# GpSimd makes the block division and the product back of a rounded feed-forward

## What is computed

```
def _mx_quantize(t, eps=1e-30):
    rows, K = t.shape
    blocks = t.reshape(rows, K // BLOCK_SIZE, BLOCK_SIZE)
    scales = jnp.maximum(jnp.max(jnp.abs(blocks), axis=-1) / FP6_E2M3_MAX, eps)
    q = _nearest_on_grid(blocks / scales[..., None], _GRID)
    return (q, scales)

x = x + _L2_xattn_ref(_layernorm(x, axis=-1), ctx_1024, mask, ...)
x = x + _L2_ffn_ref(_layernorm(x, axis=-1), L2_ffn_weight, L2_ffn_bias)
x = x + _L3_xattn_ref(_layernorm(x, axis=-1), ctx_1024, ctx_1024, ...)
```

## Time and profile before

| | us |
|---|---|
| median of 3 executions | 1220.91 (1218.79 to 1223.61) |
| the profiled execution | 1221.49 |
| its span (first to last instruction) | 1219.7 |
| PE busy | 1064.2 |
| DVE busy | 867.1 |
| ACT busy | 814.3 |
| GpSimd busy | 811.6 |

### The profile page before, as it was taken

The page is one execution under the profiler, slowest core; times in us unless marked ns, Lnnn a source line. Parts: engine busy times, 40 slices in busy tenths (PEclk is TensorE's granted clock), DMA queues, the critical chain, the costliest instruction groups (busy, mean ns, idle before and its releaser), DMA issues.

```text
span 1219.7 us, 32093 instructions
## 1 busy us (share of the span) xinstructions
PE 1064.2 (87%) x12044; PEld 880.3 (72%) x12044; DVE 867.1 (71%) x2068; ACT 814.3 (67%) x1691; POOL 811.6 (67%) x899
## 2 busy tenths in 40 slices
PE   7999896999997877787799899988778999996895
PEld 5777775999995555456588777767676777776795
DVE  8898982442226898988255587899977999986442
ACT  3577665877767989873332268877547798984573
POOL 6677788582523888678745867784346677756765
PEclk9899987999998899986899989999899999998998
DMA  6135202475326323301375400000030000001451
GB/s 214 54 113 175 55 24 80 147 215 168 105 66 193 98 80 104 97 21 49 96 227 169 99 16 15 19 26 21 17 98 27 20 28 19 28 2 53 137 155 36
DMA packets 101048, 102.59 MB, mean 84 GB/s; under 512 B 14348, under 2 KB 79120, under 8 KB 100896
## 3 DMA queue, kind: packets, MB, share of 16 engines
q1 hardware_dynamic: 90176, 78.15, 21.4%
q0 software_dynamic: 10720, 22.39, 6.4%
HBM read 57.79 MB, written 43.16 MB: 83 GB/s over the span
## 4 chain that ended last, share of the span: by engine, by line
PE 23%; DVE 11%; POOL 9%; issue 5%; ACT 3%; DMA 1%; POOLq 0%; ACTq 0%; DVEq 0%; SPq 0%
POOL F_xbuf L3016 3%; PE bP L1201 2%; POOL uni L2860 2%; PE bS L1263 2%; PE bS L1010 2%; PE bP L1019 1%; DVE mx L2339 1%; PE b L1030 1%; PE bS L859 1%; DVE uni L2151 1%; PE b L1189 1%; DVE mx L2155 1%; PE bS L1189 1%; POOL gb L3056 1%; PE bP L1278 1%
## 5 line engine op out<-in xcount | busy, mean ns | idle before, releaser
L2860 POOL TENSOR_TENSOR uni<-uni,mx 128x1024 f32<-128x1024 f32 x96 | 183.8, 1914 | 95.7 <-DVE mx L2155 65.2
L3016 POOL DMA_INDIRECT F_xbuf<-rows,idxS x128 | 132.8, 1037 | 55.3 <-issue 25.7
L2800 POOL DMA_INDIRECT gb<-F_ybuf,idxG x104 | 109.2, 1050 | 59.2 <-PE b L763 23.9
L884 PEld LDWEIGHTS b<-Vall,uni 128*64 128x64 f32 x3072 | 105.0, 144 | 42.0 <-ACT uni L1395 21.2
L884 PE MATMUL b<-Vall,uni 128*64 128x18 f32 x3072 | 110.8, 215 | 26.9 <-ACT uni L1395 14.4
L1389 ACT ACTIVATE uni<-uni 128x1024 f32<-128x1024 f32 x96 | 101.4, 1056 | 40.4 <-POOL uni L2860 39.8
L859 PE MATMUL bS<-uni,Qx 64*64 64x256 f32 x1536 | 112.2, 410 | 16.9 <-ACT uni L1352 11.1
L870 PE MATMUL bP<-k_ident,uni 128*128 128x128 f32 x768 | 110.0, 290 | 9.4 <-ACT uni L1389 9.2
L1395 ACT ACTIVATE uni<-bP 128x512 f32<-128x512 f32 x192 | 104.9, 596 | 16.2 <-PE bP L870 14.5
L870 PEld LDWEIGHTS bP<-k_ident,uni 128*128 128x128 f32 x768 | 91.0, 149 | 19.8 <-ACT uni L1389 17.3
L859 PEld LDWEIGHTS bS<-uni,Qx 64*64 64x64 f32 x1536 | 52.0, 139 | 58.7 <-issue 25.6
(11 more groups left out here) (373 smaller groups left out, 2993.2 us busy)
## 6 DMA issues: line engine op xcount, KB each, us to landing
F_xbuf<-zero SPq DMA_DIRECT2D x9, 514.0 KB, 4.9
uni<-F_xbuf SPq DMA_DIRECT2D x9, 514.0 KB, 4.7
uni<-F_xbuf SPq DMA_DIRECT2D x18, 256.0 KB, 3.4
F_ybuf<-uni SPq DMA_DIRECT2D x18, 256.0 KB
uni<-ctx_dram SPq DMA_DIRECT2D x32, 128.0 KB, 3.2
A_keys<-Qx SPq DMA_DIRECT2D x16, 256.0 KB, 2.3
uni<-A_keys SPq DMA_DIRECT2D x16, 256.0 KB
uni<-A_keys SPq DMA_DIRECT2D x32, 128.0 KB
```

The source lines that it names most:

```text
L884: ins = T.matmul(b7[64 * b:64 * b + 64, 144 * i + 18 * c:144 * i + 18 * c + 18], pPT[t % 2][:, 128 * c + 64 * b:128 * c + 64 * b + 64], pV ...
L2800: G.indirect_dma_start(gb[n], None, rows_, bass.IndirectOffsetOnAxis(ap=idxG[:, t, c:c + 1], axis=0)).then_inc(*gathered[n].up)
L2860: g.raises(G.tensor_tensor(s3, s3, mx3[t % 3][:, :].unsqueeze(2).to_broadcast([128, 16, 64]), ALU.subtract), b_sb, L, t)
L3016: G.indirect_dma_start(SP[L][0], bass.IndirectOffsetOnAxis(ap=idxS[:, t, c:c + 1], axis=0), rows3[:, t, :] if L == "F3" else XA[:, t, :], ...
```

## The change

GpSimd makes the division of each block (pool_scaled) and the product back (pool_rounded), and DVE's L2666 and L2686 are gone. Two semaphores are new: q_sc (DVE's reciprocal is there) and q_rd (DVE's last rounding step is there); q_z and q_out are now raised by GpSimd. The scales get a third buffer, am[B % 3], and DVE's scaled(B) waits for q_out(B - 3) ahead of its first instruction. Where the division and the product stood, DVE's generator has an empty step, so that its pace in A2 stays. Four tables and three calls say where in its program GpSimd does its 16 new instructions.

```
-        am = [sb(f"am{i}", [128, 64]) for i in range(2)]
+        am = [sb(f"am{i}", [128, 64]) for i in range(3)]
...
             def scaled(B):
-                z, m = steps_of(B)[0], am[B % 2]
+                z, m = steps_of(B)[0], am[B % 3]
                 d.wait_ge(f_xn, L, B)
+                d.wait_ge(q_out, L, B - 3)
...
-                n = d.tick(V.reciprocal(m[:, 32:48], m[:, 16:32]))
+                V.reciprocal(m[:, 32:48], m[:, 16:32]).then_inc(*q_sc.up)
                 yield
-                d.after(n)
-                V.tensor_tensor(blk(z), blk(z), over(m[:, 32:48]), ALU.mult).then_inc(*q_z.up)
                 yield
...
-                n = d.tick(V.scalar_tensor_tensor(a, g, MAGIC / 8.0, z, ALU.max, ALU.subtract, reverse1=True))
+                V.scalar_tensor_tensor(a, g, MAGIC / 8.0, z, ALU.max, ALU.subtract, reverse1=True).then_inc(*q_rd.up)
                 yield
-                d.after(n)
-                V.tensor_tensor(blk(g), blk(a), over(am[B % 2][:, 16:32]), ALU.mult).then_inc(*q_out.up)
                 yield
...
+        SCALED2, SCALED3 = {21: 0, 25: 1, 31: 2, 35: 3, 38: 4}, {-4: 6, -3: 7}
+        TURNED2, TURNED3 = {28: (0,), 33: (1,), 36: (2,)}, {-3: (5,), -2: (6, 7)}
+
+        def pool_scaled(g, B):
+
+            z = steps_of(B)[0].rearrange("p (n k) -> p n k", k=32)
+            g.wait_ge(q_sc, "F2", B)
+            g.alone()
+            g.raises(G.tensor_tensor(z, z, am[B % 3][:, 32:48].unsqueeze(2).to_broadcast([128, 16, 32]), ALU.mult), q_z, "F2", B)
+
+        def pool_rounded(g, B):
+
+            a, to = (t.rearrange("p (n k) -> p n k", k=32) for t in steps_of(B)[1:])
+            g.wait_ge(q_rd, "F2", B)
+            g.alone()
+            g.raises(G.tensor_tensor(to, a, am[B % 3][:, 16:32].unsqueeze(2).to_broadcast([128, 16, 32]), ALU.mult), q_out, "F2", B)
...
                 if tile(s):
                     SB(s)
+                if kind == 2 and s in SCALED2:
+                    pool_scaled(g, SCALED2[s])
+                if kind == 2 and s in TURNED2:
+                    for B in TURNED2[s]:
+                        pool_rounded(g, B)
...
         def pool_cross(g, L):
+            pool_rounded(g, 3)
+            pool_scaled(g, 5)
+            pool_rounded(g, 4)
             g.wait_ge(b_AV, "A2", NT - 1)
...
             for s in range(-8, NT + 9):
+                for B in TURNED3.get(s, ()):
+                    pool_rounded(g, B)
+                if s in SCALED3:
+                    pool_scaled(g, SCALED3[s])
```

More of the change, by code:

```diff
@@ L324, in build @@
         f_dn, f_yo = sig("f_dn", F0=NS, F1=16, F3=NS3), sig("f_yo", F0=NGF, F1=16, F3=GL3 + sum(n for _, n in GROUPS3[GL3:]))
-        q_nm, q_z, q_ab, q_out, q_Y, q_xr = (sig(n, F2=NBK) for n in ("q_nm", "q_z", "q_ab", "q_out", "q_Y", "q_xr"))
+        q_nm, q_sc, q_z, q_ab, q_rd, q_out, q_Y, q_xr = (
+            sig(n, F2=NBK) for n in ("q_nm", "q_sc", "q_z", "q_ab", "q_rd", "q_out", "q_Y", "q_xr"))
         n_fx, n_xs, n_nx = (sig(n, F3=NP) for n in ("n_fx", "n_xs", "n_nx"))
@@ L2643, in blk @@
                 return t.rearrange("p (n k) -> p n k", k=32)
-            def over(t):
-                return t.unsqueeze(2).to_broadcast([128, 16, 32])
             def offset(B):
```

## The result

| | median, us | runs | lowest to highest |
|---|---|---|---|
| kernel before | 1221.25 | 21 | 1215.62 to 1226.01 |
| changed kernel | 1225.87 | 21 | 1219.70 to 1234.09 |

The ratio is 1.0039, 95% interval 1.0022 to 1.0055: 4.6 us slower, within the 0.5% that I had called no change, and 3.5 us above the forecast of 1222.4. It is also 0.9 us above the 1220 to 1225 that I had given the forecast's own case. The profiled run of the changed kernel was the longest of its 21, 1234.09 us with a span of 1232.3, so its trace shows more than the median lost. For that reason I measure between landmarks inside the traces: from one instruction to the same one further on.

A forecast was written before the change was run, and what follows sets the result against it. GpSimd was full until A2's step 24, DVE fullest to 865 us, PE the limit in F2's tail. Division 4 +2.05, clock +1.5, block 7 -0.7 and -1.4 gave +1.45 us: 1222.4 us, range 1215.5 to 1228.

The forecast's parts named there:

- The case that I held likeliest: Whole kernel: division 4 makes PE late in F2's tail, most else is covered; +1.45 us, 1220 to 1225, chance 0.48.
- What one costs: Each new GpSimd instruction takes 1.1 us, between 0.95 and 1.28, plus 0.15 us to hand over.
- Division 0, +0.75: A2 until step 24: GpSimd's full queue makes tile 22's subtraction 0.75 us late, carried to DVE at 827.39.
- Division 1, 0.75 more at tile 26: A2 behind tile 25's subtraction: DVE's four additions wait some 0.75 us for GpSimd, lateness +1.5 at tile 26.
- Product back 0, nothing: A2: DVE saves 0.6 us before tile 28, but tile 29 hangs on tile 26's subtraction, so +1.5 stands.
- Division 2, from +1.5 to -0.6: A2 ahead of tile 31's scores: removing DVE's division, held 2.1 us, starts them and F2 0.6 us early.
- the third rival: Every GpSimd instruction holds DVE's next rounding step 1.1 us, division 2's gain is lost; about +3.6, 1224.5 us, chance 0.16.
- Division 3, +0.1: Start of F2's tail: division behind block 6's moments ends at 873.95, delaying ACT's sizes and TC(0) by 0.1 us.
- Division 4, +2.05: F2's tail: division behind block 7's moments delays ACT's sizes(4) and so PE's product 1 by 2.05 us.
- clock +1.5: PE at product 1: a wait of 2.7 us may bring back the lower clock, costing 0 to 2.2, taken as +1.5 us.
- Divisions 5 to 7, products back 3 to 6, nothing added: F2's tail: these GpSimd instructions add nothing, with 2 to 3 us of cover from PE's lateness.
- Block 7, -0.7 and -1.4: Tail's end: PE's wait for the last product back shrinks 0.7 us; product 7 at full clock saves 1.4 us.

The follow-up runs named there:

- filled2: Changed kernel plus unused PE matmuls: 6 ahead of tile 22's transposes, 14 between block 1's turning and its product; ratio 1.0041 against the kernel before.
- the control: Also written none: changed kernel with all 16 instructions back on DVE, keeping the third buffer and new semaphores; ratio 1.0009 against the kernel before.
- again: The changed kernel unaltered, timed and traced a second time; ratio 1.0047 against the kernel before.
- filled: Changed kernel plus 14 unused PE matmuls between block 1's turning and its product; ratio 1.0057 against the kernel before.
- not34: Changed kernel with the divisions of blocks 3 and 4 back on DVE; ratio 1.0037 against the kernel before.
- outonly: Changed kernel with all divisions back on DVE, only the products back on GpSimd; ratio 1.0045 against the kernel before.
- a2only: Changed kernel with only divisions 0 to 2 and products back 0 and 1 on GpSimd, the rest on DVE; ratio 1.0018 against the kernel before.
- div01: Changed kernel with only the divisions of blocks 0 and 1 on GpSimd, the other 14 instructions on DVE; ratio 1.0012 against the kernel before.
- div2: Changed kernel with only block 2's division on GpSimd, the rest on DVE; ratio 1.0016 against the kernel before.
- tailonly: Changed kernel with only divisions 3 to 7 and products back 2 to 7 on GpSimd, the rest on DVE; ratio 1.0057 against the kernel before.
- out7: Changed kernel with only block 7's product back on GpSimd, the other 15 instructions on DVE; ratio 1.0038 against the kernel before.

## Why the prediction held, and where its sum was wrong

The forecast was 1222.4 within 1215.5 to 1228.0, "within 0.5%" at 0.78; it came to 1225.87. The case that I held likeliest, division 4 late and the rest hidden, is what happened in the tail. The sum was 3.2 us short of the medians' difference (+1.45 against +4.6). That the total came out near has luck in it: the mechanism of the tail was right, that of the attention was not, and one gain was the clock's chance. Of my signs of being right, tile 31's scores a little earlier didn't come (3.1 us later), and of the signs of being wrong, a GpSimd instruction of over 1.3 us did, three times, by 0.02 us at most.

- **What one costs:** 1.05 to 1.12 us in 13 of 16, as taken.
- **Division 0, +0.75:** the lateness of tile 22 was 0.54 us. The step failed in how it carried this to tile 25, and in what it left out. It took PE for the limit there and division 1's removal for worth nothing, by a wait of 0.53 us that only the lower clock of one trace had made; with the clock kept (*filled2*) tile 25 comes 0.4 us early against the control. And it left out the clock: a longer wait of PE (1.82 for 1.27) went with a fall in 6 traces of 6, and tile 25 came 3.1 us late in the first trace, 2.4 in *again* (3.8 and 3.1 against the control). I had priced the clock at product 1, where the wait was long, and took PE here to be a fixed time behind its input.
- **Division 1, 0.75 more at tile 26:** 0.6. DVE's four additions were held as described, 1.93 us at 836.15 against 1.33 at 832.37 before, and from tile 25 to 26 it took 6.83 us in place of 6.23.
- **Product back 0, nothing:** as worked out. Tile 28 comes 0.7 us earlier after tile 27 (4.98 for 5.70), and tile 29 gives it back (6.66 for 5.93).
- **Division 2, from +1.5 to -0.6:** too large by 1.5 us. The sum took off the 2.1 us of the held division; 0.6 us came, 4.67 for 5.28 from tile 30 to 31. This is near the third rival, by which the gain at division 2 is lost: what held DVE was not a new division, though, but tile 30's subtraction, which then held the rounding step instead. The Trainium skill, page "SBUF — State Buffer", section "Who interferes with whom", says that whoever holds the shared port holds it for its whole instruction; by the 1.93 us, the trace agrees. Its +3.6 I had for the divisions in the tail; DVE's instructions did get longer there, and PE's waits at blocks 2 to 6 stayed at 0.69 us.
- **Division 3, +0.1:** ACT waited 0.43 us for it, but product 0 no longer than before (1.01 us; 1.11). Right within 0.1.
- **Division 4, +2.05, and clock +1.5:** right. The wait was 2.68 and 2.62 us (2.7), the clock's share 1.7 us by *filled*. The stretch grew by 3.5 us in place of 4.15, in which the sum had F2 start 0.6 us early.
- **Divisions 5 to 7, products back 3 to 6, nothing added:** right for the change, and only because of division 4's delay; *not34* and *outonly* show 1.7 to 1.9 us of waiting at block 5 without it, and 1.6 us of lower clock behind that.
- **Block 7, -0.7 and -1.4:** the wait for the turning shrank by 0.8 us, but product 7's own wait grew by 0.56, which leaves 0.26 of the 0.7: I hadn't followed ACT, whose four instructions of A3 stand ahead of the copy of block 7. The clock's 1.4 us is chance in both kernels: kept in 1 of 5 traces with before's waits (before, none, a2only, div01, div2), in 5 of 8 with GpSimd's and no filler there (after, again, tailonly, outonly, filled; not in not34, out7, filled2).
- **A2's end:** the 1.7 us of the first trace were 0.9 in *again*, and 0.2 in *a2only* and in the control. Not forecast; it is a longer stretch of the lower clock, and whether the change has a part in it isn't shown.

*Which half costs the median?* By one trace each the attention's share is 3.1 us against before and 3.8 against the control (64.47; 60.71), and the tail's 1.8 (after) to 3.9 (*tailonly*) against before. By medians it is the other way: with GpSimd in A2 alone 1.0012 to 1.0018, with the products back of blocks 3 to 7 on GpSimd 1.0037 to 1.0057 in all seven timings. I read this so: the kernel before loses the clock in A2 in some of its runs too, as its own trace did for some 4 us from 822 on and *div2* did, and the tail's waits are in every run. That is argued and not shown; each series of 12 runs has an interval of 0.4 to 0.7%, and only the profiled runs can be looked into. One number is on record for every run, its mean granted clock: 0.9368 over 35 runs of before, 0.9326 over the 12 of *a2only* and 0.9311 over the 21 of the change, with standard errors of 0.0006 to 0.0011. So with the attention's share alone the clock is lower over twelve runs and not in one trace only; how many us that costs, these means don't say. The two halves don't add up either: by the ratios 2.2 us and 7.0 us for the halves, 4.8 for the whole. That is barely outside the intervals, but the traces have a cause for it: the lateness from A2 covers part of the tail's, whose first two waits of PE are 4.9 us in *tailonly* and 3.7 in the change.

## What to carry to other kernels

Work moved off a full engine goes to the end of another engine's queue: place it by what stands ahead of it there and by who waits for its result, and expect that the first delay you remove shows the next one. Price every wait that grows on PE with the clock behind it, not only the long one: 0.54 us more went with up to 3.8. Before a wait in a trace is taken for the limit of a stretch, look at the granted clock in that stretch, and at a second trace where there is one: the 0.53 us here were the clock's. And an instruction held up by another engine doesn't give its hold back when it is removed, if the next one can be held too, even with one operand where the first had two.

## What the runs showed of the hardware

- Behind the same wait in the same program the granted clock fell in some traces and stayed in others: behind 1.64 us at A3's end 11.5 us of work took 16.5 at 0.59 of the clock, and behind 1.27 and 1.10 us in A2 it fell in 2 traces of 7. A single trace can differ from another by 5 us for no reason in the code, so a step must be read where it stands, and not from the span.
- GpSimd's 128x1024 subtraction held a DVE TENSOR_SCALAR with one 128x512 operand from SBUF (int32) for 1.93 us in place of 0.41, in the changed kernel and in *div2*. I had taken only instructions with two SBUF operands to be held. At 835.63, where it started 0.2 us ahead of GpSimd's division, it took 0.41 us and the division 1.12.
- A GpSimd product of 128x512 with a spread second operand takes 1.05 us, against 1.27 with two full ones.
